# Reordering the end of attention: first silus, first row loads, row transposes and routing steps

## The reference, cut to what matters

```python
x = x + attention(layernorm(x))          # causal softmax, W_O over 16 heads
t = layernorm(x)                         # 2048 tokens of 256
scores = sigmoid(t @ router.T)
idx = top8 of (scores + bias) inside the best 4 of 8 groups of experts
c = 2.5 * scores[idx] / sum(scores[idx])
x = x + sum over idx of c * (silu(t @ gate.T) * (t @ up.T)) @ down.T
      + (silu(t @ sgate.T) * (t @ sup.T)) @ sdown.T
```

## Time and profile before

| what | value |
|---|---|
| time, median of 3 | 1350.12 us |
| profiled execution | 1350.22 us |
| its span | 1348.5 us |
| PE busy | 1294.5 us (96%) |
| DVE, ACT, POOL busy | 917.6, 733.1, 572.1 us |
| granted TensorE clock | 0.992 of full speed |

### The profile page before, as it was taken

One profiled execution on the slowest core, in us unless ns is written; L12 is line 12 of the kernel. 1 busy time (PEld: TensorE's weight loads), 2 busy tenths in 40 slices (PEclk: granted clock), 3 DMA queues, 4 the chain that ended last, 5 costly groups with the idle time before them and its releaser, 6 DMA issues.

```text
span 1348.5 us, 27783 instructions
## 1 busy us (share of the span) xinstructions
PE 1294.5 (96%) x8322; PEld 1156.8 (86%) x8322; DVE 917.6 (68%) x2131; ACT 733.1 (54%) x1688; POOL 572.1 (42%) x583
## 2 busy tenths in 40 slices
PE   4999999999999999999999999999889998989998
PEld 3898888988888898878888888888778997889996
DVE  6667766677777678668878877676766742346645
ACT  2555555555555555555555555555455664556653
POOL 5526545354540313313145636542001764656574
PEclk9999999999999999999999999999999998989999
DMA  3252635525363000000001112020267997999973
GB/s 122 87 180 86 206 122 196 168 102 179 116 217 107 28 6 21 28 12 25 13 33 63 60 36 71 26 94 9 93 210 268 393 339 278 335 358 389 383 245 118
DMA packets 128265, 196.22 MB, mean 146 GB/s; under 512 B 10400, under 2 KB 99744, under 8 KB 128160
## 3 DMA queue, kind: packets, MB, share of 16 engines
q1 hardware_dynamic: 64752, 110.04, 23.8%
q10 hardware_dynamic: 51120, 51.26, 11.2%
q0 software_dynamic: 12288, 33.57, 7.1%
HBM read 107.79 MB, written 87.03 MB: 144 GB/s over the span
## 4 chain that ended last, share of the span: by engine, by line
PE 82%; DVE 7%; DMA 5%; issue 3%; ACT 2%; SPq 0%; POOL 0%; ACTq 0%; POOLq 0%; DVEq 0%
PE ps_t L852 9%; PE ps_s L796 8%; PE ps_s L798 8%; PE ps_s L797 8%; PE ps_x L796 6%; PE ps_x L798 6%; PE ps_x L797 6%; PE ps_z L796 5%; PE ps_z L798 5%; PE ps_z L797 5%; DMA ring_down<-experts_dram 4%; PE ps_t L1017 3%; PE ps_z L1017 3%; PE ps_s L986 3%; PE ps_t L796 2%
## 5 line engine op out<-in xcount | busy, mean ns | idle before, releaser
L1127 ACT ACTIVATE prob<-ps_s,neg_max 128x128 f32<-128x128 f32 (+7 forms) x256 | 190.0, 742 | 245.4 <-DVE neg_max L1325 242.3
L1340 DVE TENSOR_TENSOR pT_lo<-ps_t,pT_hi 128x512 fp32r<-128x512 f32 (+2 forms) x320 | 189.3, 604 | 88.1 <-ACT pT_hi L1143 83.7
L1143 ACT ACTIVATE pT_hi<-ps_t 128x512 fp32r<-128x512 f32 (+2 forms) x320 | 161.0, 533 | 84.7 <-PE ps_t L852 84.5
L1325 DVE CUSTOM_DVE_ANT_0 ps_s<-ps_s,causal 128x128 f32<-128x128 f32 (+7 forms) x256 | 191.1, 767 | 2.8 <-PE ps_s L798 2.4
L692 POOL DMA_INDIRECT xs<-xn,slots x128 | 129.5, 1012 | 125.0 <-PE ps_z L1017 66.3
L852 PE MATMUL ps_t<-ident,prob 128*128 128x128 f32 x1152 | 169.7, 273 | 3.0 <-ACT prob L1127 0.8
L852 PEld LDWEIGHTS ps_t<-ident,prob 128*128 128x128 f32 x1152 | 135.4, 140 | 26.9 <-issue 3.5
L796 PE MATMUL ps_s<-k_hi,q_hi 128*128 128x512 f32 (+2 forms) x384 | 142.7, 372 | 1.0 <-DVE k_lo L1318 1.0
L1537 DVE TENSOR_TENSOR h<-sg,ps_s 128x256 f32<-128x256 f32 x112 | 47.1, 420 | 134.4 <-ACT sg L1177 126.7
L796 PE MATMUL ps_s<-ring,a_hi 128*128 x384 | 127.6, 332 | 11.1 <-SPq L546 11.1
L798 PE MATMUL ps_s<-k_hi,q_lo 128*128 128x512 f32 (+2 forms) x384 | 133.5, 348 | 0.0
(11 more groups left out here) (301 smaller groups left out, 3627.6 us busy)
## 6 DMA issues: line engine op xcount, KB each, us to landing
ring<-ws SPq DMA_DIRECT2D x56, 512.0 KB, 5.9
xs<-taken SPq DMA_DIRECT2D x16, 1536.0 KB, 9.9
xq<-xs ACTq DMA_DIRECT2D x48, 512.0 KB, 7.9
xs<-yq ACTq DMA_DIRECT2D x48, 512.0 KB, 7.3
ws<-split_to SPq DMA_DIRECT2D x34, 512.0 KB, 3.1
raw<-experts_dram SPq DMA_DIRECT2D x34, 256.0 KB, 3.3
raw_a<-w_a_dram SPq DMA_DIRECT2D x15, 512.0 KB, 3.6
ring_down<-experts_dram SPq DMA_DIRECT2D x56, 128.0 KB, 7.2
```

The lines of the kernel that those rows point to most:

```text
L1127: act.activation(prob[c][:, j, 0:width(r)], ps_s[r % 2][:, 0:width(r)], ACT.Exp, bias=neg_max[:, r:r + 1], scale=-1.0, accum_out=row_sum[: ...
L1143: act.activation(to, ps_t[m % 2][:, j * P:], ACT.Copy).then_inc(s_hi, 1)
L1325: dve.tensor_tensor_reduce(out=row_of, in0=row_of, in1=causal[:, S - width(r):], scale=-1.0, scalar=LARGEST, op0=ALU.add, op1=ALU.min, acc ...
L1340: dve.tensor_tensor(lo, ps_t[m % 2][:, j * P:], hi.bitcast(F32), ALU.subtract).then_inc(s_bank_free, 1)
```

## The change

A0 and A1 are cut in two: their matmuls stay where they are, and the silu on ACT with DVE's product becomes an item H, behind the output projection W2. The first four quads of rows are issued by SP, after the last V of attention and ahead of the ring's first weights, in place of ACT at A0. The second transposes of the first token half (Y2.1) and the row transposes E4 move ahead of B0. In the list behind attention the routing items are spread with empty places ("-"): the logits L0 and L1 no longer stand side by side, Q gets a whole task between K0 and itself, and pairs of items run until step 15 in place of step 11.

The order behind W3.1 before, up to G0: N3.0 B0 A2 Y2.1 E4 N3.1 B1 C0 A3 N3.2 E5 N3.3 B2 C1 A4 Y3.0 E6 Y3.1 B3 C2 A5 L0 E7 L1 B4 C3 A6 M1 E8 G0. After: N3.0 Y2.1 E4 B0 A2 N3.1 B1 L0 C0 A3 N3.2 E5 B2 C1 A4 N3.3 E6 B3 C2 A5 Y3.0 E7 Y3.1 B4 C3 A6 E8 L1 B5 C4 A7 E9 M1 B6 C5 A8 E10 G0.

Around Q before: A11 G9 E13 K0 B10 C9 A12 Q. After: A13 G9 E15 K0 B12 C11 A14 E16 B13 C12 A15 Q. K6 stands in step 14 before and in step 17 after.

```diff
-W1.0 T2.1 R2.2 W1.1 V2.0 T2.2 R2.3 T2.3 V2.1 A0 V2.2 T3.0 V2.3 T3.1 A1 W2.0 W2.1 V3.0 T3.2 V3.1
-N2.0 T3.3 T3.4 N2.1 V3.2 T3.5 V3.3 T3.6 V3.4 T3.7 V3.5 N2.2 V3.6 V3.7 N2.3 Y2.0 W3.0 W3.1
+W1.0 T2.1 R2.2 W1.1 V2.0 T2.2 R2.3 T2.3 V2.1 A0 V2.2 T3.0 V2.3 T3.1 A1 W2.0 W2.1 H0 V3.0 T3.2 V3.1
+H1 N2.0 T3.3 T3.4 N2.1 V3.2 T3.5 V3.3 T3.6 V3.4 T3.7 V3.5 N2.2 V3.6 V3.7 N2.3 Y2.0 W3.0 W3.1
...
-    extra = items("N3.0 Y2.1 N3.1 N3.2 N3.3 Y3.0 Y3.1 L1.0 L1.1 M1")
-    extra += [("G", 1, n) for n in range(10)] + [("K", 1, 0), ("Q", 1, 0)]
+    extra = items("N3.1 L1.0 N3.2 - N3.3 - Y3.0 Y3.1 - L1.1 - M1 -")
+    extra += [("G", 1, n) for n in range(10)] + items("K1.0 - - Q1 -")
...
-    result = [extra.pop(0), ("B", 0, 0)]
+    result = items("N3.0 Y2.1 E4 B0")
     for n in range(TAIL):
-        step = step_items(n)
-        for at in (1, 3) if n < 12 else (2,):
+        step = [item for item in step_items(n) if item != ("E", 4, 0)]
+        for at in (1, 3) if n < 16 else (2,):
             if extra:
                 step.insert(at, extra.pop(0))
-        result += step
+        result += [item for item in step if item[0] != "-"]
...
+    def load_quad(engine, q):
+
+        b, i = divmod(q, PT // 2)
+        engine.dma_start(xq[q % XQ], xs[b][i * NQ:(i + 1) * NQ, :].rearrange("(t p) d -> p t d", p=P))\
+            .then_inc(s_xq[q % XQ], 16)
...
+        sp.wait_ge(s_xs[0], 16 * NT * TOPK)
         sp.wait_ge(s_pv, PV0 + NP * TRS)
+        for q in range(XQ):
+            load_quad(sp, q)
...
-            if kind == "A":
+            if kind == ("H" if g < 2 else "A"):
                 act.wait_ge(s_gu, g + 1)
...
-                if g == 0:
-                    for q in range(XQ):
-                        load_rows(q)
```

More of the change, by code:

```diff
@@ L92 @@
 W0.1 V1.0 R1.3 T1.2 T1.3 X3 V1.1 T1.4 V1.2 T1.5 V1.3 T1.6 V1.4 T1.7 V1.5 T2.0 V1.6 V1.7 R2.0 R2.1
-W1.0 T2.1 R2.2 W1.1 V2.0 T2.2 R2.3 T2.3 V2.1 A0 V2.2 T3.0 V2.3 T3.1 A1 W2.0 W2.1 V3.0 T3.2 V3.1
-N2.0 T3.3 T3.4 N2.1 V3.2 T3.5 V3.3 T3.6 V3.4 T3.7 V3.5 N2.2 V3.6 V3.7 N2.3 Y2.0 W3.0 W3.1
+W1.0 T2.1 R2.2 W1.1 V2.0 T2.2 R2.3 T2.3 V2.1 A0 V2.2 T3.0 V2.3 T3.1 A1 W2.0 W2.1 H0 V3.0 T3.2 V3.1
+H1 N2.0 T3.3 T3.4 N2.1 V3.2 T3.5 V3.3 T3.6 V3.4 T3.7 V3.5 N2.2 V3.6 V3.7 N2.3 Y2.0 W3.0 W3.1
 """
 def items(order):
-    return [(w[0], *(int(i) for i in w[1:].split(".")), *([0] * ("." not in w))) for w in order.split()]
+    return [(w[0], *(int(i) for i in w[1:].split(".") if i), *([0] * ("." not in w))) for w in order.split()]
 PROJ = [(1, "q", 0), (1, "k", 0), (1, "q", 1), (1, "k", 1),
@@ L1075, in pair @@
                     moe(kind, k)
-                else:
+                elif kind in "RTVW":
                     attend(kind, k, n, m, p, order, x_before)
@@ L1153, in load_rows @@
                 act.wait_ge(s_xs[b], 16 * NT * TOPK)
-            act.dma_start(xq[q % XQ], xs[b][i * NQ:(i + 1) * NQ, :].rearrange("(t p) d -> p t d", p=P))\
-                .then_inc(s_xq[q % XQ], 16)
+            load_quad(act, q)
         def rows_due(u):
@@ L1236, in pair @@
                     act.activation(worst_row[k], ps_x[0:1, 0:NT * TOPK], ACT.Copy).then_inc(s_x_hi, 1)
-                elif kind in "ABCE":
+                elif kind in "ABCEH":
                     moe(kind, k)
```

## The result

The changed kernel takes 1342.36 us (median of 6 runs, 1340.88 to 1344.51), the kernel before 1350.51 beside it (6 runs, 1348.94 to 1353.13). The ratio is 0.9948, with a 95% interval from 0.9935 to 0.9962: 7.0 us less, by the interval 5.1 to 8.8 (each bound's distance from 1 times 1350.5). The two medians alone differ by 8.15. The profiled execution took 1340.88, its span 1339.1, against 1350.22 and 1348.5 before.

A forecast was written before the change was run, and what follows sets the result against it. PE was taken as the bound, carrying 82% of the chain of waits. Gains of 7.5 us by the 15th task, less 0.8 given back, made 1350.2 - 6.7 = 1343.5 us; 8-in-10 range 1340.8 to 1348.0.

The forecast's parts named there:

- Part 1: Before W2: silus moved behind it remove PE's 0.8 us wait, DVE's second product costs 0.35; net gain 0.45 us.
- Part 2: Before B0: Y2.1 and E4 fill PE's 1.5 us wait for acc additions; gain 0.9 us, E4's rows landing in time.
- Part 3: At A4: first weights, queued behind 2.1 MB of rows, land at 983.2 in time; cost 0, bounds 0 and 1 us.
- Part 4: At Y3 and the logits: spacing gains 1.15 and 1.0 us; two more table loads cost 0; Y3.1's 1.0 wait stays.
- Part 5: At Q: a task between K0 and Q removes the 2.4 us wait and 1.6 of slow clock; gain 4.0 us.
- Part 6: Second scatters: POOL starts up to 8.8 us late, catches up by the 40th task; 0.8 us given back.
- the DMA engines take it back: From 1030 on: full DMA engines turn the gain into longer weight waits behind 1120; 1349 to 1350 us, chance 0.12.
- E4 waits: Before B0: rows land late, losing 3.7 us (1347.2), or 1344.7 at a single late landing; chance 0.12.
- Q still waits: At Q: DVE is later by as much as the list gives it; 4.0 us less gain, 1347.5 us, chance 0.09.
- POOL never catches up: At the second batch row's first loads: ACT waits for late scatters; slower, 1351.5 or 1353.1 us, chance 0.05.

The follow-up runs named there:

- e3: Changed kernel with both silus and their products back in A0 and A1, row loads still on SP: 1344.08 us, ratio 0.9961.
- e10: The changed kernel again, unedited, profiled anew in later rounds: 1344.39 us, ratio 0.9951.
- e5: Kernel before with only Y2.1 and E4 moved ahead of B0, rows still loaded by ACT: 1348.80 us, ratio 0.9991.
- e4: Changed kernel with the first four row loads issued by ACT behind the first silu instead of by SP: 1341.65 us, ratio 0.9932.
- e8: Changed kernel with the first four row loads behind the first two experts' weights on SP's queue: 1347.52 us, ratio 0.9986.
- e6: Changed kernel with both logits' groups side by side again: 1344.34 us, ratio 0.9956.
- e7: Changed kernel with Y3.0 and Y3.1 a task apart, L1 and M1 also later: 1340.49 us, ratio 0.9933.
- e2: Kernel before with only a whole task put between K0 and Q: 1345.87 us, ratio 0.9967.
- e1: Changed kernel with Q put back half a task behind K0: 1346.01 us, ratio 0.9972.
- e9: Changed kernel with K6 and the steps behind it, so the second scatters, four tasks later: 1345.52 us, ratio 0.9967.

## Why the prediction was right, and where its terms were not

The time was forecast as 1343.5 and came out at 1342.4 in its own rounds. The sum by the 15th task was 7.5, and 7.5 is what task 45 shows; that it agrees to the tenth is partly luck, as the terms show.

- **Part 1, 0.45: too small.** 0.84 (e3). The wait of 0.8 went, as said. The charge of 0.35 for DVE's second product was mis-sized: the waits for low parts still come to 0.7 in total, so none of it reached PE.
- **Part 2, 0.9: right in mechanism, then partly lost to the clock.** E4 did not wait. In e10 0.5 of the `acc` wait is left, where 0.6 was said. In the first profile and in e5 the clock fell to 0.74 and 0.66 from W3 on, ahead of what was moved. In the first profile that cost 0.8 (152.37 against 151.59), a term that the sum did not have.
- **Part 3, 0: right.** The first weights landed about 981.7, forecast 983.2, A4 started without waiting, and e4 fetched them 6.1 sooner for nothing. The Trainium skill, "DMA: Bandwidth & Descriptors", section "Queues, rings and completion order", says that each DMA engine takes up the descriptors of one ring in their order, though a later one may finish its write before an earlier one. e8 agrees with the order: rows issued behind two experts' weights landed at best after 6.2 us in place of 3.7.
- **Part 4, 1.15 + 1.0: right.** Y3.0 went from 1.62 to 0.43. The logits' 1.0 is 1.2 at task 8 (e6). Table loads cost nothing that shows. Y3.1's 1.0 stayed, as said, and e7 shows that it was there to take.
- **Part 5, 4.0: right.** 4.0 alone (e2), 4.7 taken out of the new list (e1). More than the 2.4 of the wait, as the clock of the earlier trace rows had told. The 0.7 between the two lists were not taken apart.
- **Part 6, 0.8 given back: not seen.** Task 47 gains 7.9, not less than task 45. PE's waits for weights from 1030 to 1135 are 4.6 us before and 5.0 after, but the gap from task 45 to 47 differs by 1.2 between the two profiles of the changed kernel alone, so 0.8 can be neither shown nor excluded. From task 45 to 111 the three profiles with the scatters in or near their old place (the kernel before, e2 and e5) need 216.3 to 217.7, the nine with the new place 214.2 to 217.4. Two readings of this part were wrong. By the table's count POOL began 1.0 earlier while the tasks came 7.5 earlier, so it was 6.5 late and not up to 8.8. And it caught up at 1113, about the 45th task, not by the 40th. The spare 0.42 was read off one late pair and held for all; in the kernel before POOL runs with gaps of 0.30 alone from 1047.80 to 1078.90, some scatters taking 1.8 in place of 0.96, and the waits of about 0.7 at every pair stand behind that.

Without the slow clock the measured terms are 0.84 + 1.0 (1.5 less the 0.5 of e10) + 1.2 + 1.2 + 4.0 = 8.24, and e10's task 45 shows 8.27. That they meet so closely is luck as well, for they were read at different tasks. With what each undoing costs at task 45 (1.3 in e3, 1.5 in e6, 4.7 in e1) and the same 1.0 and 1.2 they come to 9.7. With the 0.8 that the clock took in the first profile the 7.5 come out. Behind task 45 another 1.4 was gained up to task 111 in that pair of profiles. The stretch from task 47 to 111 takes 200.4 to 204.1 us over all thirteen profiles, in no order of the lists, so this 1.4 isn't claimed for the change.

The rivals: *the DMA engines take it back* fell, for the 47th task's gate/up starts 7.9 earlier and the engines moved 350 GB/s from 1020, where they had moved 108. *E4 waits* did not happen; e8 shows it at its price, 2.3 of wait and 1.2 to 2.1 more behind it, a total of 3.5 to 4.4, where I had 3.7. *Q still waits* fell with e2 and with the wait lists. *POOL never catches up* did not happen: POOL ran back to back until 1113 and then waited for PE again. In e4 the last scatter is in the chain, but so it is in e5, without later scatters. Where it begins to decide is not settled; e9, with four more tasks of lateness, gave 1.1 us by the medians, within the intervals.

What stays open is when the clock falls behind V3. The cluster of waits there (0.8, three short ones, and two of 0.6) stands in e10 as in the first profile, and one of the two executions fell to 0.74. Nothing in the order of the work tells them apart. Nor is it the change: up to W3 e5 has the order of the kernel before, and its clock fell, where that of the kernel before and of e2 did not.

## What to carry to other kernels

Price a stall by its length and by the clock of the stretch behind it: here 2.4 us of waiting were worth 4.0 to 4.7, and 2.3 were worth 3.5 to 4.4. The cheap cure was neither a faster producer nor fewer instructions but independent work set between producer and consumer, up to the slack that one task's 2.94 us gives. A queue's order is a choice of who waits: put first what is wanted first, even if 2.1 MB then stand ahead of a load that has slack.

## What the runs showed of the hardware that was not expected

The granted clock is not a function of the program alone. With the same order of work it was 0.74 from 975 to 980 in one execution and 1.00 in the other, behind waits of at most 0.8 us each; matmuls of W3 that start 0.12 us apart at 1.00 started 0.21 apart (974.32 and 974.53). Behind the longer wait for `seen`, 2.1 to 2.5 us, it fell in all three profiles that have this wait (0.70 before, 0.76 in e1, 0.66 in e5, from 1020 to 1025). A slow stretch can also hide a wait: the 0.5 for `acc` is absent just where the clock was low, so a wait that is missing from a list is no proof of a gain there.
